# Attention with router on one core: short query tiles placed between the next batch's long ones, and twenty tile places

## What is computed

```
q, k, v = heads(x @ wq.T) * s, heads(x @ wk.T) * s, heads(x @ wv.T)
q, k = rope(q), rope(k)
attn = softmax(q @ k^T + causal mask)                # per batch and head, 2048 x 2048
x1 = layernorm(x + (attn @ v) @ wo.T)
h = gelu([x1, mean, std, min, max, l2, sparsity] @ r1_w.T + r1_b)   # 128 wide, exact gelu
probs = softmax(h @ r2_w.T)                          # router over 32 experts, top 2, capacity 320
out = layernorm(x1 + experts(x1, probs) + adapters(x1, probs))
```

## Time and profile before

| | us |
|---|---|
| median of 3 runs | 2467.36 (2465.20 to 2468.11) |
| profiled execution | 2467.99, its span 2466.2 |
| prologue | 0 to 84.9 |
| attention, four bodies | 84.9 to 1598.3 |
| route | 1598.3 to 1893.0 |
| experts | 1893.0 to 2413.3 |
| last norm | 2413.3 to 2466.2 |

### The profile page before, as it was taken

One profiled execution on the slowest core, in us unless ns is written; L12 is line 12 of the kernel. 1 busy time (PEld: TensorE's weight loads), 2 busy tenths in 40 slices (PEclk: granted clock), 3 DMA queues, 4 the chain that ended last, 5 costly groups with the idle time before them and its releaser, 6 DMA issues. The chain is left out here.

```text
span 2466.2 us, 45555 instructions
## 1 busy us (share of the span) xinstructions
PE 2029.4 (82%) x14340; PEld 1836.2 (74%) x14340; DVE 1514.7 (61%) x3366; ACT 1335.0 (54%) x3381; POOL 789.5 (32%) x889
## 2 busy tenths in 40 slices
PE   6899998799998699999789998541145999999990
PEld 5799987698987589987679887441034999999990
DVE  6556576455666455666556666458875666666655
ACT  5566665466665366666456654210025666666655
POOL 1122332122233122233100111100048566666653
PEclk9899998799999699999789998655578999999995
DMA  1000001000000000001000000110001344455428
GB/s 57 16 16 21 18 29 33 18 18 18 27 27 27 28 12 18 25 21 33 27 12 14 20 20 27 35 51 0 0 0 41 118 140 152 150 157 152 145 71 273
DMA packets 79907, 127.51 MB, mean 52 GB/s; under 512 B 15652, under 2 KB 69904, under 8 KB 75628
## 3 DMA queue, kind: packets, MB, share of 16 engines
q1 hardware_dynamic: 63852, 114.99, 13.6%
q0 software_dynamic: 15872, 10.24, 2.5%
HBM read 100.29 MB, written 35.65 MB: 55 GB/s over the span
## 5 line engine op out<-in xcount | busy, mean ns | idle before, releaser
L458 PE MATMUL out_ps<-v_sb,probs_t 128*128 128x64 f32 x4352 | 559.7, 274 | 45.9 <-DVE probs_t L749 35.5
L458 PEld LDWEIGHTS out_ps<-v_sb,probs_t 128*128 128x128 f32 x4352 | 540.8, 196 | 55.5 <-DVE probs_t L749 52.5
L735 DVE TENSOR_REDUCE part_max<-scores_ps 128x1 f32<-128x512 f32 (+3 forms) x576 | 357.4, 622 | 299.1 <-PE scores_ps L426 234.1
L426 PE MATMUL scores_ps<-k_st,q_parts 128*128 128x512 f32 (+3 forms) x1280 | 418.9, 411 | 23.8 <-POOL q_parts L863 14.4
L605 ACT ACTIVATE probs<-scores_ps,neg_max 128x512 f32<-128x512 f32 (+3 forms) x640 | 397.4, 626 | 61.1 <-DVE neg_max L739 46.8
L614 ACT COPY probs_t<-probs_t_ps 128x512 f32<-128x512 f32 (+3 forms) x416 | 208.7, 502 | 282.5 <-PE probs_t_ps L443 281.5
L443 PE MATMUL probs_t_ps<-ident,probs 128*128 128x128 f32 x2176 | 352.8, 278 | 2.3 <-DVE probs_t L749 2.2
L443 PEld LDWEIGHTS probs_t_ps<-ident,probs 128*128 128x128 f32 x2176 | 265.4, 144 | 54.4 <-issue 6.4
L1464 PE MATMUL up_ps<-xe_t,w 128*128 128x320 f32 x1920 | 289.3, 310 | 2.1 <-DVE xe_t L1571 1.7
L1464 PEld LDWEIGHTS up_ps<-xe_t,w 128*128 128x128 f32 x1920 | 284.0, 189 | 2.7 <-issue 1.9
L885 POOL TENSOR_TENSOR rstd<-mean_var,power 128x1 f32<-128x1 f32 x64 | 37.8, 590 | 618.9 <-DVE mean_var L791 618.9
(11 more groups left out here) (219 smaller groups left out, 3221.5 us busy)
## 6 DMA issues: line engine op xcount, KB each, us to landing
w_raw<-in_w_expert SPq DMA_DIRECT2D x32, 1536.0 KB, 6.5
w_raw<-in_w_adapter SPq DMA_DIRECT2D x32, 384.0 KB, 7.1
x_t<-in_x_t SPq DMA_DIRECT2D x64, 128.0 KB, 2.1
x_row<-in_x SPq DMA_DIRECT2D x64, 128.0 KB, 2.0
x_rows<-x SPq DMA_DIRECT2D x64, 128.0 KB, 1.7
acc_rows<-x SPq DMA_DIRECT2D x64, 128.0 KB, 1.8
ln_x<-acc_rows SPq DMA_DIRECT2D x16, 512.0 KB, 6.1
out_rows_dram<-ln_y SPq DMA_DIRECT2D x16, 512.0 KB, 5.2
```

Of the source, the lines that this page charges most:

```text
L426: mm = pe.matmul(out, q_parts[:, s % 2, part_, h, :], k_st[:, h, lo:hi], start=part_ == 0, stop=part_ == 1 and not diagonal)
L458: mm = pe.matmul(o_ps[:, h, :], probs_t[:, g % PT_RING, a - lo:a - lo + P], v_sb[:, a // P, h, :], start=a == 0, stop=a == t * P)
L735: red = dve.tensor_reduce(neg_max[:, ring:ring + 1] if single else part_max[:, ring, c:c + 1], s_ps[:, bank[g], 0:hi - lo], AX.X, ALU.max, ...
```

## The change

- All 64 tiles are one list, written out by tile_order(): batch 0 has its tiles 15 to 4; in batches 1 to 3 the four short tiles of the batch before stand ahead of tiles 15, 13, 11 and 9; in the last batch its own tiles 3, 2, 1 and 0 stand after tiles 8, 7, 6 and 5, so that tile 4 is last. All loops over batches become straight code, waits become constants.
- k_st, q_t, v_sb and cos_sin get twenty tile places: the short tiles of odd batches live in places 16 to 19. The prologue projects 20 tiles (batch 0, and batch 1's tiles 0 to 3). Slot m then projects the 20th next: for a long tile the same tile of the next batch, for a short one that of the batch after the next. The last 20 slots project nothing.
- SHORT_ROUNDS and the bank set aside go; ROUNDS serves all slots. A short tile and the long tile behind it share their chunks: the steps of the first are spread over the first half, those of the second over the second. Where a batch's tile 3 comes up, the first three rounds stand at its first chunk. sums and norm are taken out of the rounds and stand at each tile's start. attn gets two buffers.
- PE waits for k_lower and v_copied only where a chunk first needs newer keys or values; ACT's split of q waits for q_copied.
- Router rows leave SBUF: ACT copies them to a small buffer hidden (two places), SP stores each pair of tiles with two DMAs to a DRAM tensor, and route loads all of it into hpre with 16 DMAs ahead of the experts' weights. ACT's gelu waits for the loads of its group.

```diff
@@ ROUNDS, attention_slots @@
-    (("sums", 1), ("norm", 1), ("qt", 1)),
+    (("qt", 1),),
...
-SHORT_ROUNDS = (
-    (("sums", 1), ("norm", 1), ("qt", 1), ("x1t", 2)),
-    (("qt_read", 1), ("x1t_read", 2), ("kt", 1), ("ot", 1)),
-    (("kt_read", 1), ("ot_read", 1), ("proj", 0), ("wo", 1), ("hidden", 2)),
-    (("hidden_read", 2), ("wo_read", 1), ("ln", 1), ("proj_read", 0), ("rope", 0), ("v", 1)),
-    (("v_read", 1), ("x1", 1), ("xt", -1)),
-    (("stats", 1), ("dup", 0)),
-)
-ASIDE = ("qt", "kt", "proj", "v")
+PROJECTION = ("qt", "kt", "proj", "v", "rope", "xt", "dup")
+def tile_order(NB, NT):
+
+    order = []
+    for b in range(NB):
+        long = list(reversed(range(4, NT)))
+        fill = [(b - 1, t) for t in (3, 2, 1, 0)] if b else []
+        for n, t in enumerate(long):
+            if fill and n in (0, 2, 4, 6):
+                order.append(fill[n // 2])
+            order.append((b, t))
+            if b == NB - 1 and 7 <= n < 11:
+                order.append((b, 10 - n))
+    return order
+
+
+def attention_slots(NB, NT):
+
+    order = tile_order(NB, NT)
+    count = len(order)
...
+    span = [(start[m], start[m + 1]) for m in range(count)] + [(total, total + 2)] * 2
+    m = 0
+    while m < count - 1:
+        if order[m][1] < 4 <= order[m + 1][1]:
+            half = (start[m] + start[m + 2]) // 2
+            span[m], span[m + 1] = (start[m], half), (half, start[m + 2])
+            m += 1
+        m += 1
+
+    projected = NT + 4
     early, late = ([[] for _ in range(total + 3)] for _ in range(2))
     at, made = 0, {}
-
-    short = start[max(tiles - 4, 0)]
-    late[0].append(("xt", 0, None))
-    for s in range(tiles + 2):
-        n = start[s + 1] - start[s] if s < tiles else 2
-        rounds = ROUNDS if start[min(s, tiles)] < short else SHORT_ROUNDS
-        for r, steps in enumerate(rounds):
-            offset = r * (n - 1) // (len(rounds) - 1)
-            at = min(max(at, start[min(s, tiles)] + offset), total + 2)
+    late[0].append(("xt", projected))
+    for s in range(count + 2):
+        lo, hi = span[s]
+        if 1 <= s <= count:
+            early[start[s]].append(("sums", s - 1))
+            late[start[s]].append(("norm", s - 1))
+        for r, steps in enumerate(ROUNDS):
+            offset = r * (hi - lo - 1) // (len(ROUNDS) - 1)
+            if r < 3 and s < count and order[s][1] == 3 and order[s][0] < NB - 1:
+                offset = 0
+            at = min(max(at, lo + offset), total + 2)
             for k, back in steps:
-                of, when = s - back, None
-                if of >= tiles:
+                of = s - back
+                if k.removesuffix("_read") in PROJECTION:
+                    of += projected
+                    if not projected <= of < NB * NT:
+                        continue
...
@@ attention @@
+    COUNT = NB * NT
+    FIRST = NT + 4
...
+    def slot(b, t):
+
+        return NT + t if t < 4 and b % 2 else t
+
+    projected = [(n // NT, n % NT) if n < FIRST else
+                 (order[n - FIRST][0] + (2 if order[n - FIRST][1] < 4 else 1), order[n - FIRST][1])
...
-        def misc(kind, s):
-
-            return s_ps[:, AHEAD - 1, :] if (kind, s) in aside else m_ps[:]
...
-        k_st = sb("k_st", [P, HEADS, S], F32R)
+        k_st = sb("k_st", [P, HEADS, FIRST * P], F32R)
-            with eng.Fori(0, NT // 2 - 1) as j:
+            with eng.Fori(0, FIRST // 2 - 1) as j:
...
+            def store_hidden(j):
+
+                sp.wait_ge(hid_copied, ONE + j + 1)
+                for a in range(2):
+                    m = 2 * j + a
+                    sp.dma_start(dram["hidden"][:, row(m):row(m) + P], hidden[:, j % 2, a, :])\
+                      .then_inc(hid_stored[j % 2], 16)
+
+            for m in range(COUNT):
+                n = FIRST + m
+                if n < COUNT:
+                    b, t = projected[n]
+                    load_xt(n, n % 2, b * NT + t, n - 1)
+                if m >= 2:
+                    sp.wait_ge(resid_done, ONE + m - 1)
+                sp.dma_start(x_row[:, m % 2, :], dram["x"][row(m):row(m) + P, :]).then_inc(xrow_loaded[m % 2], 16)
+                if m >= 2:
+                    store(m - 2)
+                if m >= 4 and m % 2 == 0:
+                    store_hidden(m // 2 - 2)
+            for m in (COUNT - 2, COUNT - 1):
+                store(m)
+            for j in (COUNT // 2 - 2, COUNT // 2 - 1):
+                store_hidden(j)
             for r in range(2):
-                sp.wait_ge(x1_stored[r], 32 * (NT // 2) * NB)
+                sp.wait_ge(x1_stored[r], 16 * COUNT)
+                sp.wait_ge(hid_stored[r], 8 * COUNT)
...
+                if latest_key(g) >= keys_seen[0]:
+                    keys_seen[0] = latest_key(g) + 1
+                    pe.wait_ge(k_lower, ONE + keys_seen[0])
...
+                if latest_key(g) >= values_seen[0]:
+                    values_seen[0] = latest_key(g) + 1
+                    pe.wait_ge(v_copied, ONE + values_seen[0])
...
+            def split_q(m):
+
+                act.wait_ge(scores_ready, ONE + first_chunk[HEADS * max(m - 1, 0)])
+                act.wait_ge(q_copied, ONE + nth_projected[order[m]] + 1)
+                act.copy(q_parts[:, m % 2, 0], q_t[:, :, cols(*order[m])]).then_inc(q_upper, 1)
...
+                elif kind == "hidden_read" and k % 2:
+                    j = k // 2
+                    act.wait_ge(hid_done, j + 1)
+                    if j >= 2:
+                        act.wait_ge(hid_stored[j % 2], 32 * (j // 2))
+                    act.copy(hidden[:, j % 2].rearrange("p a b -> p (a b)"), m_ps[:, D:2 * D]).then_inc(hid_copied, 1)
...
+                    if k >= 2:
+                        dve.wait_ge(attn_turned, ONE + k - 1)
+                    dve.tensor_tensor(attn[:, r].rearrange("p (h d) -> p h d", h=HEADS), o_ps[:],
+                                      norm_by[:, r].to_broadcast([P, HEADS, HD]), ALU.mult).then_inc(attn_ready, 1)
...
@@ gpsimd @@
-                    elif kind == "rope" and more and ("proj", k) not in aside:
+                elif kind == "rope":
+                    pool.wait_ge(rope_mul, ONE + k + 1)
+                    rope_sums(pool, products, roped).then_inc(roped_ready, 1)
...
@@ route @@
+        hpre = sb("hpre", [P, NTT * P])
+            for b in range(NTT // 16):
+                for g in range(G):
+                    part = slice((g * TG + 4 * b) * P, (g * TG + 4 * b + 4) * P)
+                    sp.dma_start(hpre[:, part], dram["hidden"][:, part]).then_inc(hid_loaded[b], 16)
+                act.wait_ge(hid_loaded[b], 16 * G)
```

751 lines of the change are left out of this document (347 added, 404 removed).

## The result

| | before | after |
|---|---|---|
| median, us (four runs each, same chip) | 2466.56 | 2375.48 (2373.59 to 2377.30) |
| profiled execution, us | 2467.99 | 2373.83, span 2371.9 |
| ratio of the times | | 0.9632, 95% interval 0.9619 to 0.9644 |

What follows compares the result with a forecast made beforehand. TensorE bounds long tiles; batch ends lose idle PE and clock. Back 128.6 - 36 - 6.3 + 11.2 + 23.9 = 121.4, paid 16.7 + 6.5 = 23.2, net 98.2 us: 2369 us, forecast case 2350 to 2395, overall range 2325 to 2430.

Steps and rivals of the forecast that it cites:

- The dents: Batch ends, short tiles to next batch's start: 128.6 us lost to idle PE and lower clock, all recoverable if joints were free.
- the 11.2 of the moved projections: Interleaved part: four tiles' projections leave for the prologue, each costing 2.8 us beside PE-bound work, so 11.2 us back.
- Joints at 3 us a pair: Tile changes in front of batches 1 to 3's long tiles: waits for attn and first exponential, twelve pairs, 36 us stay lost.
- rival A: Free joints: the long neighbour always gives PE work, joints and hand-offs cost nothing, last pairs half; 2318 us, chance 0.16.
- Rival D: Slower than before: every short tile carries its loss along, only the paid items are left; 2486 us, chance 0.03.
- the term of 23.9: Batch 3's tiles 7 to 0: of 41.9 us lost, 18 stay, 4.5 per pair, so 23.9 us come back.
- rival B: Joints take the clock along: each pair idles PE 4.3 us, then runs partly at 1.2 GHz; 2437 us, chance 0.21.
- Four more tiles in the prologue: Prologue: projecting batch 1's first 512 keys with nothing beside it costs 4.18 us each, 16.7 us for four.
- Ropes on POOL: New profile: POOL's rope products for 44 tiles instead of 36, DVE's for the other 20; waits behind DVE's rope gone.
- Router rows: 6.5 forecast: End of attention and route start: last store 2.6 us on the path, gelu 3.9 later for reloads, 6.5 us paid.
- Loops to straight code at 0: Batch loops: straight code and constant waits change 0 us, since looped code fills PE to 97%; at most 3%.
- C, the chain of steps: Shared misc bank: no slot shorter than 18.0 us, pairs of tiles 11 and 9 take 36 each; 2387 us, chance 0.06.

Runs made afterwards that it cites:

- the mixed run: The changed kernel with the last batch's tiles 7 to 4 and 3 to 0 between tiles 15 to 8, tiles 0, 4, 8 last: 2363.72 us.
- the fastest version: The changed kernel with the last batch mixed, first value product one chunk later in the last 20 slots only, gelu table load ahead of its wait: 2357.53 us.
- the run before it: The changed kernel with the last batch mixed, first value product one chunk later in all batches, gelu table load ahead of its wait: 2369.02 us.

## Why the forecast came close, step by step

The net was 98.2 us and became 94.3 in the profiled runs. That hides two errors of opposite sign: the batch stretches gave 11.7 us more than forecast (109.2 against 97.5) and the last eight tiles 15.1 less (8.8 against 23.9). The profiled run of after lies 1.7 us under its median where that of before lay 0.6 above the one I used; with the 4.0 us of the profiled runs (2373.8 against 2369.8) that is the 6.5 between 2369.0 and 2375.5.

**The dents: right that most comes back.** Three stretches lost 128.6 us. They became 109.2 shorter, 98.0 without the 11.2 of the moved projections; the forecast had 86.3. After, PE is idle for 15.5 us in 16 slots at clock 1.00; eleven long tiles of before have 7.4 us, so the twelve in these slots would have an estimated 8.1. About 7.4 us are left to four pairs, 1.9 each with the hand-offs at tile 3. The rest of the 10.3 us that stay lost in this stretch (41.0 less 30.7) is 2.2 us of PE's busy time above the work that I had reckoned.

**Joints at 3 us a pair: right in kind of size, wrong in place.** I had priced waits for attn and for the first exponential, from the earlier trace rows. At out_ps the trace shows 0.9 us for four pairs, and at the scores nothing from ACT: rival A's free joints, as far as these go. What costs are the misc bank's hand-offs, q_t 6.1, x_ts 3.0 and k_st 2.4 us in 16 slots, of which eleven long tiles of before already have 2.7, 0.5 and 0. I had counted them only where a batch's tile 3 comes up, 2.1 us a time, and there they are as forecast, 0.68 + 1.40 in batches 1 and 2 (1.91 in batch 3):

```profile
761.67 0.66 PE L380 MATMUL misc_ps<-ident,roped 128*128 128x128 f32 x4 [0.68 <-ACT q_t L565]
763.73 1.66 PE L368 MATMUL misc_ps<-w_qkv,x_t_parts 128*128 128x512 f32 x6 [1.40 <-DVE k_st L710]
```

So A was right on the joints of batches 1 and 2. Its 2318 was too low since it left the hand-offs out and put the loss of the last pairs at 9 us, where 33.1 were lost.

**What brings the gain: wrong reason.** I named the restarts and the rope. With both gone and the chunks not shared the time is that of before (2474) and 9.3 of the 98.0 us come back in the three stretches, and the rope's move in the kernel before brings nothing. The sharing of a pair's chunks carries the rest, and of the shares tried the half is best; the forecast mentioned the sharing in one sentence and priced nothing on it. That its sum came close all the same is luck in part. Rival D, at 0.03, had the right mechanism for a kernel without that sharing.

**The last eight tiles: the term of 23.9 was mis-sized.** I let 18 us stay lost, 4.5 a pair. Idle PE is exactly that, 18.0. What I left out is the clock: 97.80 us of busy time at 0.85 is 14.7 us more in the window 1363.1 to 1478.9, and the two make 32.7 of the 115.8 - 82.7 = 33.1 us that stayed lost. This is rival B, which had put 3.1 to 4.6 a pair on it, true in this one stretch: 3.7 a pair. In batches 1 and 2, with four pairs in each, it is false, the granted clock being 1.00; in batch 3's long part, with four more, the clock is 0.98:

```profile
1115.90:1363.10 247.20, 237.96 (x1823) 213.73 (x1823) 160.48 (x419) 149.90 (x438) 30.34 (x36) 0.98 0.08 24
```

In the 16 slots no hole of PE is longer than 1.40 us; in the last eight tiles the longest is 2.63:

```profile
1433.45 1.08 PE L474 MATMUL out_ps<-v_sb,probs_t 128*128 128x64 f32 x8 [2.63 <-DVE attn L773]
```

In the mixed run, with a hole of 2.99 us, the last 20 slots keep 0.97, so the longest hole doesn't settle the clock either. The Trainium skill (TensorE: Matmul & The Clock Gate, HAM oscillation) describes a kernel whose clock fell again at every tile, where PE waited for a DMA. No run here has such waits: the clock fell to 0.85 in the last eight tiles over holes of up to 2.63 us behind DVE.

**Four more tiles in the prologue: right.** 16.7 forecast, 15.6 measured. **Ropes on POOL: right.** The rope's last sums on POOL (44 tiles) and on DVE (the 20 of the prologue) over the whole run:

```profile
L904 POOL TENSOR_TENSOR roped<-products 128x256 f32<-128x256 f32 x44 | 32.2, 733 | 3.1
...
L905 DVE TENSOR_TENSOR roped<-products 128x256 f32<-128x256 f32 x20 | 18.3, 916 | 0.0
```

**Router rows: 6.5 forecast, 8.0 measured.** The store ahead of the barrier took 2.1, near the 2.6. The data was there 7.1 us after the barrier (6.4 forecast): 1 MB landed 6.2 us after its first load was issued, where I had worked out 5.6. The other 1.3 is a step that I had overlooked: ACT's table load of 1.28 us. In before it ran in front of the wait for b_r (1.21 us); now it follows the wait for the rows:

```profile
1598.35 1.28 ACT L1064 ACT_TABLE_LOAD   x1 [0.54 <-PEq L189]
```

Made ahead, as in the fastest version, the gelu starts 7.5 us after ACT reached route, against 8.4. The Trainium skill (ScalarE: Activation LUTs, What ACT_TABLE_LOAD costs) has 1283 ns for the instruction, and the trace agrees. The rule cited in the forecast, of the Trainium skill (DMA: Bandwidth & Descriptors, Anatomy of one DMA), is a fit for DMAs that GpSimd issues; its estimate of 4.4 us is too short for these loads of SP, which took 6.2.

**Loops to straight code at 0: not tested apart.** Batch 0's long tiles take 266.2 us before and 266.1 after, but they were straight code in both. In the kernel before, eleven long tiles took 266.2 us as straight code (batch 0) and 269.5 in the loop, with 5.8 and 7.4 us of idle PE; batch 0 makes fewer router rows in that stretch, so the loop's share is at most these 3.3 us a batch, for two batches. What of it was gained is part of the 9.3 us above. **C, the chain of steps:** in the shape I gave it, no; yet that shares of 7 and of 12 chunks both cost suggests that such a chain stands just behind PE.

What stays open: whether a second place for out_ps would free the joints at no cost elsewhere, what a restart between batches costs by itself, and what sets the clock when many small holes stand in a stretch. None of these was tried.

## What to carry to other kernels

When short work is laid between long work, what pays is that the short one's dependent steps get matmuls of a neighbour at every hand-off; the place in the order alone brought 9 of 98 us here. So count the steps with one buffer, give each a slice of other work, and try shares on both sides: 7, 10 and 12 of 20 chunks were 76 and 29 us apart. Price an idle hole with its clock, and take the clock from several executions: spreading 26 us of holes went with 8.5 us less busy time, but one and the same code differed by 6.4. And ask what is late next: a wait taken away in one place (the rope, the later product) came back in another.

## What the runs showed of the hardware

- Granted clock against holes: 15.5 us idle in 353.8 left it at 1.00; 28.5 in 373.2 gave 0.99; 32.0 in 381.7 gave 0.97; 27.2 in 363.0 gave 0.94, and 25.8 in 353.1, spread, 0.97. The fastest version has 0.95 with 19.0 in 350.3, and the same code in the run before it 0.97 with 20.3 in 345.1, so the sum of the holes alone does not tell the clock.
- Sixteen loads of 256 KB were issued in 8.60 us, 0.54 each, and the first four, 1 MB, released their reader 6.2 us after the first was issued.
- ACT's table load (1.28 us) runs where its first use stands; behind a wait it adds to it, and in the fastest version an activation of one column ahead of the wait moved it out.
